# Routing in four groups and a slot table in DRAM: a graph layer with a mixture of experts on one Trainium2 core

## The chip, the core and the metric

The kernel runs on one core of a Trainium2 chip. A core has engines with an instruction queue each: TensorE (PE, whose weight loads the profile lists as PEld), VectorE (DVE), ScalarE (ACT), GpSimd (POOL) and SyncE (SP), and 16 DMA engines. The metric is the time of one execution on the device, in microseconds; of several executions the median is taken.

## What is computed

6250 nodes carry 256 features each. With `xn` the layer-normed input, the kernel adds three things to `x`:

```
x = x + gnn(xn, src, dst) + mix(xn)        # 206250 edges; mix: linear attention, 8 heads
x = x + ffn(layernorm(x))                  # mixture of 8 experts, capacity 977 each

# in ffn
logits = x @ gate_w + gate_b
idx    = argmax(softmax(logits));  prb = that probability
pos    = (cumsum(one_hot(idx), axis=0) * one_hot).sum(-1) - 1      # place within the expert
kept   = pos < C
buf[idx, pos] = x ;  y = relu(buf @ w1 + b1) @ w2 + b2
out    = y[idx, min(pos, C-1)] * (prb * kept)
```

Only the part that finds `idx`, `prb` and `pos` of each node, and the table from an expert's slots back to nodes, is what follows calls **routing**. `pos` is a running count over all nodes, so routing has an order.

## The kernel before, in words

Nodes lie in 49 blocks of 128; two blocks are a **pair** (`q`), 24 pairs and a last block of 106. The program has three stages: one with layer norm, keys and values and the degrees (to about 375 us), the **main stage** (about 378 to 1119 us), and the experts (from about 1140 us).

**Main stage.** For each destination block the neighbours' rows are summed by one-hot matrices. Each block takes 16 **slots**. In every slot PE builds four tiles (`build`, L1680, from marks that DVE wrote), ACT evacuates them (`tile_evac`, L1277), and PE sums the tiles of the block before with six or eight matmuls (`sum_up`, L1688). DVE writes the marks in four chunks per block (two instructions each at L1964), up to twelve slots before PE needs them; a ring holds them. In slot 2 of each block PE also transposes the next block's keys (`block_keys`, L1626), which makes these rows a clock of the stage: one per block.

Four blocks, those of the pairs 8 and 16 (`GATHERED`), are not summed by PE. GpSimd gathers their neighbours' rows by indirect DMA and lets the DMA add them up: per pair 56 rounds for two blocks, 112 DMAs, the first four without an addition (L974), the others with one (L976). All 224 stand back to back in GpSimd's queue. Four accumulators take turns, so that a gather waits only for the one four before it. DVE picks the sums up in `gathered` (L2251, L2255), in its fixed place. So 45 blocks remain on PE, at the positions 0 to 44, and DVE reaches pair 8's sums at position 18, pair 16's at position 32, each at slot 8 of the block.

Beside the blocks, each pair is **finished**: in slots 0 to 15 after its start (`first`) the mix matmuls (PE, L1554), scaling, bias and norm (DVE), in slots 16 to 31 (`second`) the second layer norm, its transposes (L1768) and the gate matmuls. `finish_starts` spaces the starts by 32 slots, but by 24 behind the gathered pairs, since two blocks less lie between them: pairs 8 to 12 and 16 to 20 come denser. This holds in the branch `sparse`, taken when no block has more than its share of edges; it is the one that runs here.

**Routing, per pair** (before):
- `choose` on DVE, seven instructions (L2393 to L2400): logits from the gate's PSUM, bias, maximum, difference, first best expert, one-hot.
- ACT's `exps` (L1357), with a load of its table.
- PE's `count` (L1786 to L1789): running counts by matmuls with a triangle of ones.
- `route` on DVE, sixteen instructions (L2415 to L2442): probability, position, slot number, and then one-hot rows of the slot's low and high part.
- PE's `place` (L1795): two matmuls spread node number and probability into a table `inv_ps` in PSUM.
- `add_slots` on DVE (L2409) adds this to `inv_acc`.

PE waits for `inv_added` before it writes keys to the PSUM bank that also holds `inv_ps` and `cum_ps`. All engines run in program order; a wait holds up what stands behind it.

**Tail.** Behind position 44, the last block and the last pair are routed together (three blocks wide, `last_route`). Then `inv_acc` gives the experts' lists of nodes.

## Time and profile before

| | us |
|---|---|
| median of 3 runs | 1460.66 |
| lowest, highest | 1456.71, 1464.74 |
| the profiled execution | 1463.94 |
| its span, first to last instruction | 1462.7 |
| PE, DVE, ACT, POOL busy | 1305.0, 1198.4, 934.8, 799.2 |
| granted TensorE clock, mean | 0.970 |

The busy share of an engine counts the modelled duration of each instruction. A matmul's includes its way through the array, and matmuls overlap, so that 98% busy does not mean full use. A stretch of the program is read better from the times between rows that come once per block. "Idle before <-" names what ended an engine's wait.

### The profile page before, as it was taken

How to read it: one execution, taken by the hardware profiler on the slowest of the kernel's cores; microseconds unless marked ns; L12 is line 12 of the kernel's file. 1: busy time of each engine (PE TensorE's matmuls, PEld its weight loads, DVE VectorE, ACT ScalarE, POOL GpSimd, SP SyncE). 2: the span in 40 equal slices, each digit the busy share in tenths (PEclk: the TensorE clock that was granted, in tenths of full speed). 3: DMA queues.
4: the chain of work that ended last, by engine and by line, in shares of the span. 5: the costliest groups of instructions: out<-in, count | busy, mean ns of one | idle time of the engine just before them, and what ended most of it. 6: DMA issues, size and time to landing. Idle time of an engine off the chain costs nothing. (4 is left out here: it accounts for less than half of the span.)

```text
span 1462.7 us, 38776 instructions
## 1 busy us (share of the span) xinstructions
PE 1305.0 (89%) x14051; PEld 1091.4 (75%) x14053; DVE 1198.4 (82%) x2455; ACT 934.8 (64%) x2122; POOL 799.2 (55%) x629
## 2 busy tenths in 40 slices
PE   4698888995879999998989998999999898989987
PEld 3355555562768888887878887888886687979986
DVE  7797888898869888998899888989984577767786
ACT  4486777776546676665756666657665556565754
POOL 5357445206238888888888884000000577676574
PEclk8799999997989999999999999999999999999999
DMA  9625431002826655666655664121114433343220
GB/s 301 209 57 118 93 77 37 29 23 93 255 64 114 120 99 99 99 99 131 107 105 122 108 101 75 38 73 38 38 38 138 126 118 122 95 136 116 74 79 25
DMA packets 96441, 145.71 MB, mean 100 GB/s; under 512 B 14249, under 2 KB 72262, under 8 KB 96123
## 3 DMA queue, kind: packets, MB, share of 16 engines
q0 software_dynamic: 46080, 69.85, 26.0%
q1 hardware_dynamic: 50186, 73.61, 15.1%
q8 instruction: 100, 1.64, 0.5%
q14 instruction: 75, 0.61, 0.2%
HBM read 105.08 MB, written 60.14 MB: 113 GB/s over the span
## 5 line engine op out<-in xcount | busy, mean ns | idle before, releaser
L1688 PE MATMUL bank<-reg_b,reg_a 128*128 128x256 f16 x4410 | 597.3, 275 | 8.5 <-ACT reg_a L1277 8.0
L1277 ACT ACTIVATE reg_a<-bank 128x392 f16<-128x392 f32 x720 | 343.0, 496 | 214.7 <-PE bank L1680 187.2
L1688 PEld LDWEIGHTS bank<-reg_b,reg_a 128*128 128x128 f16 x4410 | 396.8, 98 | 51.0 <-issue 10.2
L976 POOL DMA_INDIRECT reg_a<-h_rows,reg_d x216 | 395.1, 1829 | 66.2 <-issue 66.2
L1964 DVE TENSOR_TENSOR reg_c<-iota_v,reg_c 128x2048 f16<-128x2048 f16 (+1 forms) x282 | 368.2, 1321 | 45.3 <-ACT reg_c L1170 15.6
L1680 PE MATMUL bank<-reg_a,reg_c 128*128 128x98 f16 x2880 | 243.0, 209 | 16.1 <-ACT reg_a L1277 10.2
L1680 PEld LDWEIGHTS bank<-reg_a,reg_c 128*128 128x128 f16 x2880 | 200.4, 99 | 32.4 <-issue 17.4
L1964 DVE TENSOR_TENSOR reg_a<-iota_h,reg_c 128x1568 f16<-128x1568 f16 x180 | 174.3, 968 | 0.0
L990 POOL COPY take_idx<-inv_i 128x8 int32<-128x8 int32 (+1 forms) x8 | 1.7, 217 | 240.5 <-DVE inv_i L2515 240.5
L1920 PE MATMUL bank<-w_hi,hid_hi 128*128 128x256 f32 (+1 forms) x368 | 107.3, 292 | 12.1 <-DVE w_lo L2550 6.9
L1922 PE MATMUL bank<-w_hi,hid_lo 128*128 128x256 f32 (+1 forms) x368 | 104.6, 284 | 0.0
L1921 PE MATMUL bank<-w_lo,hid_hi 128*128 128x256 f32 (+1 forms) x368 | 104.5, 284 | 0.0
L1901 PE MATMUL bank<-xT_hi,w_hi 128*128 128x512 f32 (+2 forms) x240 | 85.5, 356 | 9.6 <-issue 5.5
L1035 POOL DMA_INDIRECT out<-reg_d,give_idx x60 | 71.7, 1195 | 40.8 <-issue 20.8
L1432 ACT ACTIVATE reg_d<-reg_d,slot_prb 128x256 f32<-128x256 f32 (+1 forms) x46 | 22.6, 506 | 103.2 <-DVE reg_d L2590 100.5
L2034 DVE TENSOR_REDUCE reg_e<-reg_e 128x16 f32<-128x1040 f32 x49 | 60.4, 1233 | 34.1 <-ACT reg_e L1148 32.2
L871 POOL DMA_INDIRECT reg_b<-in_dst,row_i x49 | 58.4, 1193 | 54.0 <-PE bank L1484 26.2
L995 POOL DMA_INDIRECT reg_b<-tok_rows,take_idx x64 | 75.6, 1182 | 17.7 <-issue 11.5
L1902 PE MATMUL bank<-xT_lo,w_hi 128*128 128x512 f32 (+2 forms) x240 | 81.1, 338 | 0.0
L1903 PE MATMUL bank<-xT_hi,w_lo 128*128 128x512 f32 (+2 forms) x240 | 81.0, 338 | 0.0
L1920 PEld LDWEIGHTS bank<-w_hi,hid_hi 128*128 128x128 f32 (+1 forms) x368 | 70.0, 190 | 14.6 <-issue 4.9
L1554 PE MATMUL bank<-reg_w,xnT_t 128*128 128x512 f16 x300 | 73.1, 393 | 4.1 <-issue 1.9
(370 smaller groups left out, 2520.6 us busy)
## 6 DMA issues: line engine op xcount, KB each, us to landing
reg_b<-in_L_ffn_w SPq DMA_DIRECT2D x16, 1024.0 KB
h_rows<-reg_b POOLq DMA_DIRECT2D x14, 896.0 KB, 9.8
tok_rows<-reg_e SPq DMA_DIRECT2D x24, 512.0 KB
x_bias<-in_x SPq DMA_DIRECT2D x1, 6250.0 KB
x_bias<-b_out_rows POOLq DMA_DIRECT2D x10, 625.0 KB
x_t<-x_bias SPq DMA_DIRECT2D x24, 256.0 KB
xnT_t<-xnT_rows SPq DMA_DIRECT2D x24, 256.0 KB
out<-reg_e SPq DMA_DIRECT2D x24, 256.0 KB
```

Source lines behind the costliest of these rows:

```text
L976: ins = g.indirect_dma_start(out=acc[i % 2][m][k], out_offset=None, in_=h_rows, in_offset=at, compute_op=ALU.add)
L995: nc.gpsimd.indirect_dma_start(out=gx[k][:, c, :], out_offset=None, in_=tok_rows[:, :], in_offset=bass.IndirectOffsetOnAxis(ap=take_idx[k] ...
L1277: return a.activation(AT[k].rearrange("p h (w t) -> p h w t", w=2)[:, :, :, s * GROUP:(s + 1) * GROUP], tile_ps[bk][:, 0:GROUP * 2 * NB].r ...
L1680: ins = t_.matmul(tile_ps[bk][:, i * 2 * NB:(i + 1) * 2 * NB], lo_ring[c][:, s % CG * GROUP + i, :], hi_ring[c][:, s % CG * GROUP + i, :], ...
L1688: ins = t_.matmul(agg_ps[k][:, 0:D], AT[k][:, h, :], h_all[:, half, h, :], start=(first and h + half == 0), stop=(last and h == NB - 1 and ...
L1901: t_.matmul(bank[f % 4][:, 0:w], w1_hi[:, c, fs], xT_hi[:, c, at], start=(c == 0), stop=False)
L1902: t_.matmul(bank[f % 4][:, 0:w], w1_hi[:, c, fs], xT_lo[:, c, at], start=False, stop=False)
L1903: ins = t_.matmul(bank[f % 4][:, 0:w], w1_lo[:, c, fs], xT_hi[:, c, at], start=False, stop=(c == DC - 1))
L1920: t_.matmul(y_ps, hid_hi[:, f, at], w2_hi[:, f, :], start=(f == 0), stop=False)
L1921: t_.matmul(y_ps, hid_hi[:, f, at], w2_lo[:, f, :], start=False, stop=False)
L1922: ins = t_.matmul(y_ps, hid_lo[:, f, at], w2_hi[:, f, :], start=False, stop=(f == FC - 1))
L1964: return v_.tensor_tensor(out.rearrange("p t (v u) -> p t v u", u=2), iota.rearrange("p (v u) -> p v u", u=2).unsqueeze(1).to_broadcast(sh ...
```

## The change

- `choose` is cut down per pair: DVE only multiplies the gate's PSUM out into a buffer `logits` for all blocks (`gate_out`).
- The rest runs in four groups: pairs 0 to 7, 8 to 15, 16 to 21, and 22 alone. `group_choose` and `group_route` on DVE are instructions up to 16 blocks wide; ACT has one `exps` per group, PE one chain of counting matmuls. The first three groups stand at positions 19, 33 and 43 (`group_pos`): choose at slot 0, ACT's exp at slot 6, count and route at slot 8.
- `place` and `add_slots` per pair are gone, with the one-hot rows for them. In their place DVE computes a row number, and GpSimd writes for each block 128 rows of two numbers (node and probability, 8 bytes) to a table `slot_rows` in DRAM by an indirect DMA (`scatter`, 46 in all).
- GpSimd's 16 scatters of the first group stand inside the gathers of pair 16, those of the second and third behind the gathers, the last two in the tail.
- The table in DRAM is zeroed early from `inv_acc`; SP loads it back (`slot_tab`) once all scatters have landed, and `add_slots` adds it to the last three blocks' `inv_ps` once.

```diff
-FIN_STEPS = ROUTE_STEPS + MIX_STEPS + 6
+FIN_STEPS = MIX_STEPS + 1
+GROUP_STEPS = 17
+ROUTES = ((0, 8), (8, 16), (16, 22), (22, 23))
...
+GATHER_FROM = 40
+GATHER_SLOTS = 2.3
+SCATTER_LATE = 32
...
+    slot_rows = dram("slot_rows", (NE * CROWS, 2))
...
+    GROUP_AT = GroupAt(0, 6, 8, 8)
+    group_pos = [-(-(starts[q1 - 1] + 2 * SLOTS) // SLOTS) for _, q1 in ROUTES[:-1]]
...
     # SyncE
+        sp.wait_ge(inv_added, 1)
+        sp.dma_start(slot_rows.rearrange("(p c) w -> p (c w)", p=P), inv_acc[:, :]).then_inc(xb_in, 16)
...
         load_b2(0, 0)
+        sp.wait_ge(placed, 16 * 2 * (NQ - 1))
+        sp.dma_start(slot_tab, slot_rows.rearrange("(p c) w -> p c w", p=P)).then_inc(w_in2, 16)
         finished(NQ)
...
     # GpSimd
+        def scatter(b):
+            g.indirect_dma_start(out=slot_rows, out_offset=bass.IndirectOffsetOnAxis(ap=slot_row[:, b:b + 1], axis=0),
+                                 in_=token[:, b, :], in_offset=None, bounds_check=NE * CROWS - 1, oob_is_err=False
+                                 ).then_inc(placed, 16)
+
+        def group(i):
+            pool.wait_ge(slot_hot, i + 1)
+            for b in range(2 * ROUTES[i][0], 2 * ROUTES[i][1]):
+                scatter(b)
...
                 for j in range(GROUNDS):
                     for m in range(2):
+                        at_slot = GATHER_FROM + GATHER_SLOTS * ((i * GROUNDS + j) * 2 + m)
+                        if (scattered < len(ROUTES) - 1 and group_pos[scattered] * SLOTS + SCATTER_LATE < at_slot
+                                and (group_pos[scattered] + 1) * SLOTS < starts[q]):
+                            group(scattered)
+                            scattered += 1
...
+            for i in range(scattered, len(ROUTES) - 1):
+                group(i)
...
     # ScalarE
-            if s == 15:
-                exps(q)
+                def fin(s):
+                    if s == GROUP_AT.exps and p in group_pos:
+                        group(group_pos.index(p))
...
     # TensorE
-            if s == 5 and not first_pair(q):
-                pe.wait_ge(key_out, min(q * 2 + 5, NB) if isinstance(q, int) else q * 2 + 5)
-                pe.wait_ge(inv_added, q)
-                count(q - 1)
...
+        def group(i, keys=None):
+            w = 2 * (ROUTES[i][1] - ROUTES[i][0])
+            pe.wait_ge(key_out, min(keys or 2 * ROUTES[i][1] + 3, NB))
+            pe.wait_ge(route_hot, i + 1)
+            t_.matmul(cum_ps[:, 0:w, :], utri16[:, :], g_hot[:, 0:w, :], start=True, stop=False)
+            for d in range(1, w):
+                t_.matmul(cum_ps[:, d:w, :], ones16[:, :], g_hot[:, 0:w - d, :], start=False, stop=False)
+            t_.matmul(cum_ps[:, 0:w, :], ones16[:, :], g_routed[:, 0:w, :], start=False, stop=True).then_inc(route_cum, 1)
...
         def tail():
-            for s in (5, 6):
-                first(NQ - 1, s)
+            first(NQ - 1, 6)
+            group(len(ROUTES) - 1)
...
     # VectorE
             if c == 3:
                 dve.wait_ge(fin_gate, q + 1)
-                choose(q, q)
+                v_.tensor_tensor(logits[:, ds(q * 2, 2), :], gate_ps, mix_bc[:, D:DG].unsqueeze(1).to_broadcast([P, 2, NE]),
+                                 ALU.mult).then_inc(gate_out, 1)
...
+            group_step(v_.scalar_tensor_tensor(low, low, float(NE * CT), high, ALU.mult, ALU.add))
+            group_step(v_.tensor_tensor(slot_row[:, b0:b1], low, drop, ALU.add))
+            dve.sem_inc(slot_hot, 1)
...
+        def add_slots():
+            dve.wait_ge(w_in2, 96)
+            dve.wait_ge(slot_used, 2)
+            halves_ = inv_acc[:, :].rearrange("p (w c) -> p w c", w=2)
+            v_.tensor_tensor(halves_, slot_tab.rearrange("p c w -> p w c"),
+                             inv_ps.rearrange("p (w c) -> p w c", w=2), ALU.add).then_inc(inv_added, 1)
```

**Where instructions move.** GpSimd, the gathers of the main stage, before (the first two rows are pair 8, the others pair 16):

```order
L974 DMA reg_a<-h_rows,reg_d 128x256 x4
L976 DMA reg_a<-h_rows,reg_d 128x256 x108
L974 DMA reg_a<-h_rows,reg_d 128x256 x4
L976 DMA reg_a<-h_rows,reg_d 128x256 x108
```

And in the changed kernel, the same place:

```order
L1016 DMA reg_a<-h_rows,reg_d 128x256 x4
L1018 DMA reg_a<-h_rows,reg_d 128x256 x108
L1016 DMA reg_a<-h_rows,reg_d 128x256 x4
L1018 DMA reg_a<-h_rows,reg_d 128x256 x13
L970 DMA slot_rows<-reg_c 8192x2 x16
L1018 DMA reg_a<-h_rows,reg_d 128x256 x95
L970 DMA slot_rows<-reg_c 8192x2 x28
```

Sixteen scatters have come between the 17th and the 18th gather of pair 16, and 28 stand behind the last one.

DVE, position 19 of the changed kernel (L2009 are the marks, L2280 scales a block's sum), the choosing half of the first group:

```order
L2280 SCALAR_TENSOR_TENSOR reg_e<-bank,rin,norm_bc 128x256
L2445 COPY reg_c<-routed 128x128
L2446 TENSOR_TENSOR reg_c<-reg_c,gate_b_bc 128x128
L2447 TENSOR_REDUCE reg_c<-reg_c 128x16
L2448 TENSOR_TENSOR reg_c<-reg_c 128x128
L2450 SCALAR_TENSOR_TENSOR reg_c<-reg_c,rev 128x128
L2451 TENSOR_REDUCE reg_c<-reg_c 128x16
L2452 TENSOR_TENSOR reg_c<-rev,reg_c 128x128
L2454 TENSOR_REDUCE reg_c<-reg_c 128x8
L2455 TENSOR_TENSOR routed<-routed,reg_c 128x8
L2009 TENSOR_TENSOR reg_c<-iota_v,reg_c 128x2048
```

These nine stand between two chunks of marks; the eleven of the routing half stand two chunks later, before the last layer norm steps of pair 8. Before, 16 instructions of `route` stood in front of the norm of every pair.

## Rows read from the trace of the kernel before

**Rows 1.** Windows: length, busy us (x instructions) of PE, PEld, DVE, ACT, POOL; PEclk, DMA, GB/s.
```profile
600.00:650.00 50.00, 49.20 (x610) 44.75 (x609) 44.34 (x105) 34.39 (x74) 42.99 (x24) 1.00 0.73 111
700.00:750.00 50.00, 45.68 (x535) 40.96 (x533) 45.18 (x107) 32.82 (x72) 42.39 (x26) 0.97 0.62 118
```
**Rows 2.** Who waited for whom, 500 to 1100 us: us in total, times, longest.
```profile
PE bank L1680 <- ACT reg_a L1277: 7.7, 4, 2.2
...
ACT reg_e L1345 <- DVE reg_e L2352: 7.4, 4, 2.1
```
**Rows 3.** Groups by line: busy us, mean ns of one | idle us before them.
```profile
L976 POOL DMA_INDIRECT reg_a<-h_rows,reg_d x216 | 395.1, 1829 | 66.2 <-issue 66.2
...
L1035 POOL DMA_INDIRECT out<-reg_d,give_idx x60 | 71.7, 1195 | 40.8 <-issue 20.8
```
**Rows 4.** Timeline of DVE: the pick-up of the gathered sums of pairs 8 and 16.
```profile
668.42 0.43 DVE L2251 TENSOR_TENSOR reg_a<-reg_a 128x256 f32<-128x256 f32 x1 [3.24 <-issue]
...
901.06 0.43 DVE L2251 TENSOR_TENSOR reg_a<-reg_a 128x256 f32<-128x256 f32 x1 [2.60 <-DMA reg_a<-h_rows,reg_d]
903.43 0.43 DVE L2251 TENSOR_TENSOR reg_a<-reg_a 128x256 f32<-128x256 f32 x1 [1.94 <-DMA reg_a<-h_rows,reg_d]
```
**Rows 5.** Timeline of POOL: a gather, two plain ones, and the last of all.
```profile
617.06 1.54 POOL L976 DMA_INDIRECT reg_a<-h_rows,reg_d  x1 [0.31 <-issue]
...
663.99 1.71 POOL L974 DMA_INDIRECT reg_a<-h_rows,reg_d  x1 [0.30 <-issue]
666.00 0.95 POOL L974 DMA_INDIRECT reg_a<-h_rows,reg_d  x1 [0.30 <-issue]
...
895.93 1.92 POOL L976 DMA_INDIRECT reg_a<-h_rows,reg_d  x1 [0.31 <-issue]
```
**Rows 6.** Timeline of DVE, 600 to 635 us: start, length, line, operation.
```profile
605.40 0.17 DVE L2393 TENSOR_TENSOR reg_e<-bank,mix_bc 128x16 f32<-128x16 f32 x1 [0.88 <-PE bank L1554]
...
606.78 1.22 DVE L1964 TENSOR_TENSOR reg_c<-iota_v,reg_c 128x2048 f16<-128x2048 f16 x1
...
615.25 0.17 DVE L2415 TENSOR_REDUCE reg_e<-reg_e 128x2 f32<-128x16 f32 x1
...
618.63 1.22 DVE L1964 TENSOR_TENSOR reg_c<-iota_v,reg_c 128x2048 f16<-128x2048 f16 x1
...
624.48 0.25 DVE L2409 TENSOR_TENSOR inv_acc<-inv_acc,bank 128x128 f32<-128x128 f32 x1
```
**Rows 7.** Timeline of PE, 600 to 642 us, with three key rows.
```profile
608.24 0.25 PE L1626 MATMUL bank<-ident,reg_c 128*64 128x64 f16 x4
...
615.50 1.47 PE L1554 MATMUL bank<-mix_hl,xnT_t 128*128 128x256 f16 x12
616.80 0.34 PE L1680 MATMUL bank<-reg_a,reg_c 128*128 128x98 f16 x4
...
621.20 0.61 PE L1795 MATMUL bank<-reg_w 128*128 128x128 f32 x4
621.65 0.34 PE L1680 MATMUL bank<-reg_a,reg_c 128*128 128x98 f16 x4
...
624.79 0.25 PE L1626 MATMUL bank<-ident,reg_c 128*64 128x64 f16 x4 [0.72 <-DVE inv_acc L2409]
...
639.65 0.25 PE L1626 MATMUL bank<-ident,reg_c 128*64 128x64 f16 x4
```
**Rows 8.** Timeline of PE: key rows (L1626) of the positions 20, 24, 34, 38.
```profile
692.98 0.32 PE L1626 MATMUL bank<-ident,reg_c 128*64 128x64 f16 x4
...
764.67 0.25 PE L1626 MATMUL bank<-ident,reg_c 128*64 128x64 f16 x4 [1.30 <-DVE inv_acc L2409]
...
927.77 0.25 PE L1626 MATMUL bank<-ident,reg_c 128*64 128x64 f16 x4
...
999.99 0.25 PE L1626 MATMUL bank<-ident,reg_c 128*64 128x64 f16 x4 [1.30 <-DVE inv_acc L2409]
```
**Rows 9.** Timeline of DVE in the tail: scaling of the last block.
```profile
1121.29 0.48 DVE L2235 SCALAR_TENSOR_TENSOR reg_a<-bank,rin,norm_bc 128x256 f32<-128x256 f32 x1 [0.37 <-DVE reg_a L2361]
```

More of the change, by code:

```diff
@@ L512, in build @@
     gs_of = [g_s if q in (0, NQ - 2, NQ - 1) or q % 2 == 0 else g_alt for q in range(NQ)]
-    Places = namedtuple("Places", "mix count route place add")
-    KEYS_AT = 2
-    PLACES = {2: Places(9, 9, 8, 14, 12), 14: Places(9, 9, 8, 16, 16), 10: Places(9, 11, 12, 18, 20),
-              6: Places(9, 9, 8, 14, 12)}
+    KEYS_AT, MIX_AT = 2, 9
+    GroupAt = namedtuple("GroupAt", "choose exps count route")
+    GROUP_AT = GroupAt(0, 6, 8, 8)
+    group_pos = [-(-(starts[q1 - 1] + 2 * SLOTS) // SLOTS) for _, q1 in ROUTES[:-1]]
+    gs_of = [g_s if q in (0, NQ - 2, NQ - 1) or q % 2 == 0 else g_alt for q in range(NQ)]
+    KEYS_AT, MIX_AT = 2, 9
+    GroupAt = namedtuple("GroupAt", "choose exps count route")
+    GROUP_AT = GroupAt(0, 6, 8, 8)
+    group_pos = [-(-(starts[q1 - 1] + 2 * SLOTS) // SLOTS) for _, q1 in ROUTES[:-1]]
     def places_of(q):
-        return PLACES[(KEYS_AT - starts[q]) % SLOTS]
+        return Places(9, 11, 12) if (KEYS_AT - starts[q]) % SLOTS == 10 else Places(9, 9, 8)
     def active(p, s):
@@ L525, in active, with main_phase @@
         return [(q, at - starts[q]) for q in range(NQ - 1) if 0 <= at - starts[q] < 2 * SLOTS]
-    def main_phase(eng, gnn, prepare, first, second, tail, sparse, ahead=None):
+    def main_phase(eng, gnn, prepare, first, second, tail, sparse, group, ahead=None):
         def blocks(with_rounds):
@@ L541, in pairs @@
             pair(0)
-            with eng.Fori(1, NQ - 2) as q:
-                pair(q)
+            for i, (q0, q1) in enumerate(ROUTES[:-1]):
+                with eng.Fori(max(q0, 1), q1) as q:
+                    pair(q)
+                group(i)
             pair(NQ - 2)
@@ L1754, in first @@
                 ins.then_inc(fin_mix, 1)
-            if s == 14 and not first_pair(q):
-                place(q - 1)
         def second(q, s):
             w, o = blocks_of(q), fin_of(q)
-            if s == -1:
-                pe.wait_ge(inv_added, q + 1)
             if s == 10:
@@ L1822, in tail @@
             busy(7)
-            pe.wait_ge(route_hot, NQ)
-            t_.matmul(total_ps, ones16[:, :], routed[:, :], start=True, stop=False)
-            for m in range(3):
-                t_.matmul(total_ps, ones16[:, :], last_route.hot[:, m, :], start=False, stop=(m == 2))
-            count(NQ - 1, 3, last_route)
+            last_count()
             busy(12)
-            pe.wait_ge(inv_added, NQ)
-            place(NQ - 1, 3, last_route)
+            last_place()
             busy(30)
@@ L2328, in first @@
                 biased(q, *(sums or ()))
-                if not sums:
-                    slots_of_last(q)
+                n[0] = 0
             if c == 3:
-                if not first_pair(q) and not fixed(q, NQ) and not sums:
-                    add_slots(q - 1)
                 if not fixed(q, NQ):
@@ L2411, in route, with each @@
-        def route(p, q, w=2, o=pair_route):
+            def each(part):
+                return part.unsqueeze(2).to_broadcast([P, w, NE])
+            dve.wait_ge(gate_out, ROUTES[i][1])
+            v_.tensor_copy(g_routed[:, 0:w, :], wide(routed[:, :]))
+            group_step(v_.tensor_tensor(log, log, wide(gate_b_bc[:, :]), ALU.add))
+            group_step(v_.tensor_reduce(out=top, in_=log, op=ALU.max, axis=AX.X))
+            v_.tensor_tensor(diff, log, each(top), ALU.subtract).then_inc(route_d, 1)
@@ L2446, in tail @@
             link(v_.tensor_scalar(node_1[:, NB - 1:NB], node_1[:, NB - 1:NB], valid[:, :], None, ALU.mult))
-            for c in (0, 1, 3):
+            for c in (0, 1):
                 first(NQ - 1, c)
+            group(len(ROUTES) - 1)
+            first(NQ - 1, 3)
             for c in (0, 1):
@@ L2458, in tail @@
             dve.wait_ge(fin_gate, NQ + 1)
-            choose(NQ - 1, NQ, 3, last_route)
-            route(NQ - 1, NQ, 3, last_route)
-            add_slots(NQ - 1)
+            last_choose()
+            last_slots()
+            add_slots()
         def sparse():
@@ L2496, in fin @@
                             second(q, at // CG - CHUNKS, True)
-                        if at == places_of(q).add and q:
-                            add_slots(q - 1)
                 gnn(b, p % 2, fin, False, DENSE[p + 2] if p + 2 < len(DENSE) else None)
-        main_phase(dve, gnn, prepare, first, second, tail, sparse)
-        dve.wait_ge(inv_added, NQ + 1)
-        n_inv = [0]
+        main_phase(dve, gnn, prepare, first, second, tail, sparse, group)
+        dve.wait_ge(inv_added, 2)
+        n_inv = [len(ROUTES) * GROUP_STEPS]
         def chain(ins):
             n_inv[0] += 1
-            ins.then_inc(inv_dve, 1)
-            dve.wait_ge(inv_dve, n_inv[0])
+            ins.then_inc(slot_dve, 1)
+            dve.wait_ge(slot_dve, n_inv[0])
         in_slot = inv_acc[:, 0:NE * CT]
```

233 lines of the change are left out of this document (136 added, 97 removed).

## The prediction

> **What bounds the kernel now.** I read the windows of the main stage first, then one pair on DVE and on PE, then what GpSimd delivers and who waits for it.
>
> In a regular stretch PE is busy 49.2 of 50 us, DVE 44.3 [rows 1]. In the dense stretch behind a gathered pair PE falls to 45.7 of 50 while DVE rises to 45.2, and the granted clock to 0.97 of 2.4 GHz [rows 1]. So PE sets the pace where pairs start 32 slots apart, and where they start 24 apart DVE's lateness gets through: ACT waits for DVE's variances (L1345, up to 2.1 us) and PE for ACT's tiles (L1680, up to 2.2 us) [rows 2].
>
> A third engine matters. GpSimd's 224 gathers run without a gap: each takes 1.83 us, with 0.31 us of issue ahead of it, 2.13 us in all [rows 3]. DVE waits for them at both places where it picks up sums: 3.2 us for pair 8, until 668.4, and for pair 16 from 898.5 to 903.4, 2.6 and 1.9 us in two waits [rows 4]. The last gather left GpSimd at 897.85 and landed 5.6 us later [rows 4, 5]. So both meetings are already late by a little: **whatever DVE and PE gain ahead of a meeting is lost there, and whatever is put into GpSimd's queue ahead of the last gather moves the second meeting.**
>
> **What goes.** On DVE `choose` takes 1.38 us (605.40 to 606.78, seven instructions, 0.20 each) and `route` 3.38 us (615.25 to 618.63) [rows 6]. One instruction of `choose` stays; with `add_slots` 1.2 + 3.4 + 0.2 = 4.8 us go per pair, some 105 us over 22 pairs. On a regular pair that is worth nothing by itself, since PE paces it. PE loses `count` (five narrow matmuls, an estimated 0.13 us), `place` (0.45 us, 621.20 to 621.65) and its wait for `inv_added` before the keys (0.72 us, at 624.79): 1.3 us per regular pair [rows 7]. ACT loses an Exp and its table load per pair, hidden.
>
> **What comes.** A group costs DVE 20 chained instructions. Small ones are 0.20 us; the wide ones 0.25 to 0.30 us, as for L2409's 128 columns (0.25) [rows 6]: some 2.4 us for choosing and 2.6 us for routing. PE gets 17 narrow matmuls, an estimated 0.5 us, ACT one table load there and back. For the third group DVE has lead enough, so only PE's 0.5 us count. The first and second stand at positions 19 and 33, right behind a meeting, when DVE has no lead: their 5 us use up the 4.8 us that pair 8 (or 16) no longer costs there. So I take the time from the meeting to the key row of position 20 (668.4 to 693.0) as it is, less 0.5 us, and likewise from the second meeting to position 34 (903.4 to 927.8) [rows 4, 8]. PE will wait at slot 8 of these positions for the first one-hots; the same wait was ACT's and PE's before.
>
> **The dense stretches, behind the groups.** Positions 20 to 24 take 71.7 us [rows 8]. A regular pair with its two positions takes 31.4 us (608.24 to 639.65), 30.1 without its 1.3 us [rows 7]. Four positions with two pairs would be 60.2 us; at 24 slots apart it is two thirds of a pair more, whose matmuls (mix 1.30 us [rows 7], gates and transposes an estimated 0.7) add 1.3: 61.5 us. DVE, with 4.8 us less per pair, needs about 0.84 us per slot against PE's 0.95, so PE paces; I leave 1.0 us for waits and take 62.5 us: 9.2 us gained. Positions 34 to 38 (72.2 us) gain the same.
>
> **The sum, against the profiled execution (1463.94 us).**
> 1. Up to 668.4 us: seven pairs gain 9.1 us, and all of it goes into a longer wait of DVE at the first meeting. 0.
> 2. Position 20 to 24: −9.2. Position 24 to 32: four pairs at 1.3, and 0.6 more where the wait was 1.30 (764.67): −5.8 [rows 8]. With item 1's 0 DVE is at the second meeting 15.0 us earlier, 883.5 instead of 898.5 us.
> 3. GpSimd: 16 scatters inside pair 16's gathers. **This price the trace does not show**; nearest is the indirect store of 128 rows in the expert stage, 1.20 + 0.30 = 1.50 us [rows 3]. Lower bound: a plain gather with DVE at rest, 0.95 + 0.30 = 1.25 us; upper bound: a gather with addition, 2.13 us [rows 3, 5]. At 1.50 they are 24.0 us, and the last gather would be issued at 921.9.
> 4. But DVE then stands still from 883.5. A gather that no marks disturb takes 1.54 us instead of the mean 1.83; a plain one took 1.71 us under marks and 0.95 in DVE's wait [rows 3, 5]. Spacing 1.84 instead of 2.13 is 0.136 less: 38.4 us shrink by 5.2, and the longer first wait gives 1.0. The second meeting comes 24.0 − 5.2 − 1.0 = 17.8 us later, at 921.
> 5. Behind it: −9.2 to position 38; to the end 3.5 pairs at 1.3 and a wait of 0.5: −5.0; the third group's matmuls +0.5.
> 6. Tail: PE waits about 2.7 us for the one-hots of pair 22 before it sums the last block, but DVE comes to scale that block about 2 us after PE is done, held by its own work [rows 9]: +0.3. The reload of the table (64 KB) hides behind the expert's weights: 0; if the last scatters landed late, the experts would start late by as much.
>
> 17.8 − 9.2 − 5.0 + 0.8 = **+4.4 us: 1468.3 for the profiled execution**, which stands 3.3 us above the median; for the median 1460.66 + 4.4 = **1465 us**. With s for a scatter's price the sum is 13.8 × s − 16.4: it turns at s = 1.19 us, gives +1 at 1.25, and is over +0.5% (7.3 us, what a measurement of this kernel can tell) from s = 1.71; at 2.13 it is +13.
>
> **A rule against the trace.** During `route` (615.25 to 618.63) GpSimd is not slowed: the gather that starts at 617.06 takes 1.54 us [rows 5, 6]. The Trainium skill (SBUF — State Buffer, the note on the "DVE blocks DMA" trap in "two separate sides") says that GpSimd cannot write descriptors while DVE holds the port pair they share, and gives about 0.62 us for such a DMA alone and 3.1 us beside a DVE copy. It agrees with item 4, and speaks against scatters amid marks: by its 3.1 us they would be 50 us, an estimate from that page; the trace's plain gather under marks lost 0.8 us against the one at rest, not 2.5 [rows 5].
>
> **Rivals.**
> - **A, slower: the scatters cost as the gathers with addition.** Sixteen at 1.71 to 2.13 us and more, because they fall at 696 to 730 us, where DVE writes marks densely, or because the small writes delay the landings of the gathers behind them. +7 to +13, 1468 to 1474. It decides from 1.71 us. For it: 1.71 us for a plain gather under marks [rows 5]. Against: the mean of 60 stores, 1.20 us. Chance 0.2.
> - **B, faster: the scatters cost GpSimd little**, since each moves 1 KB where a gather moves 128. At s = 0.3 to 0.7 the sum is −12 to −7, about 1451. For it: nothing moves twice through memory. Against: a plain gather at rest still takes 0.95 us, and no indirect DMA in the trace less [rows 5]. Chance 0.12.
> - **C, faster: the lighter DVE lets GpSimd gather faster throughout.** If routing held it up as marks do (15% of the time before 898, 0.29 of 1.83 us), 11 us would go: −7, about 1454. Against: the undisturbed gather during `route`. Chance 0.08.
> - **The change does not do what it says:** the three groups on DVE take as long as the 22 pairs. They cannot: some 15 against 105 us.
>
> **How the numbers follow.** My case has 0.6: 1461 to 1468 by the scatter's bounds up to 1.71, and ±4 us for the stretches that I estimated. Of it I count 0.13 as slower by over 0.5% and 0.01 as faster, the rest within. A adds 0.2 to slower, B and C 0.14 to faster and 0.06 within. Faster 0.15, within 0.5% 0.52, slower 0.33. The range takes in B's and A's middles: 1450 to 1476.
>
> **What would show it.** In the new profile: 16 scatters between 696 and about 720 us, their mean and gap; gathers ending near 916 instead of 898; DVE's wait at the first meeting about 12 us, at the second about 38, with PE idle some 30 us before 924; gathers at 1.54 us meanwhile; the key row of position 24 near 755, of 38 near 1008; regular pairs 1.3 us shorter, without L1626 waiting. I am wrong if DVE does not wait for GpSimd at position 32, or if the gathers end where they ended before.

## The result, and the profile after

The change takes **1477.49 us** (median, 1476.61 to 1478.74); the kernel before took 1461.97 us in the same measurement (1456.71 to 1464.74). The ratio is 1.011, 95% interval 1.008 to 1.014: slower by 15.5 us, where +4.4 was forecast, and just outside the range (1450 to 1476). The profiled execution spans 1475.4 us against 1462.7, its mean granted clock is 0.950 against 0.970.

The page of the change, busy time and the slices:

```profile
span 1475.4 us, 37910 instructions
PE 1311.6 (89%) x13895; PEld 1085.5 (74%) x13896; DVE 1122.9 (76%) x2007; ACT 886.7 (60%) x2065; POOL 851.4 (58%) x675
PE   5688999986899999988799996899988899989987
PEclk8799999996999999999799997899999999999999
```

A slice is 36.9 us. PE falls to 7 tenths, from 8 in the slice before, and the clock to 0.7, in the one that begins at 701 us; the 6 at 885 us holds the second meeting, and the 8 behind it (922 to 959 us) a second fall that no meeting explains. The windows of the main stage, as in [rows 1], and then the stretches around two places that the forecast did not have (length, busy us of PE, PEld, DVE, ACT, POOL; PEclk, DMA share, GB/s):

```profile
600.00:650.00 50.00, 50.00 (x615) 45.60 (x613) 38.36 (x69) 31.12 (x74) 42.46 (x25) 1.00 0.63 115
700.00:750.00 50.00, 38.74 (x405) 31.73 (x404) 32.05 (x59) 22.95 (x53) 42.08 (x27) 0.79 0.47 84
...
692.00:707.00 15.00, 7.11 (x42) 3.37 (x41) 5.62 (x12) 2.35 (x8) 11.65 (x12) 0.67 0.02 1
707.00:718.00 11.00, 4.48 (x22) 2.23 (x22) 1.58 (x2) 2.77 (x6) 9.17 (x7) 0.50 0.43 58
...
945.00:956.00 11.00, 6.77 (x44) 3.57 (x43) 3.37 (x4) 1.52 (x5) 7.74 (x7) 0.71 0.02 2
```

In a regular stretch all is as forecast: PE is full, DVE is down from 44.3 to 38.4 of 50 us. But from 692 to 718 us PE issues 64 matmuls in 26 us, where it has 211 in the 18 us that follow. DVE and ACT are mostly idle with it (7.2 and 5.1 us busy of the 26), and until 707 us the DMA engines too (0.02); only GpSimd works. PE's timeline there (start, length, line, operation, idle time before it and what ended it):

```profile
700.58 0.24 PE L1733 MATMUL bank<-reg_a,reg_c 128*128 128x98 f16 x1 [1.00 <-issue]
700.62 0.41 PE L1741 MATMUL bank<-reg_b,reg_a 128*128 128x256 f16 x1
702.00 1.01 PE L1741 MATMUL bank<-reg_b,reg_a 128*128 128x256 f16 x4 [0.96 <-issue]
703.47 0.37 PE L1741 MATMUL bank<-reg_b,reg_a 128*128 128x256 f16 x1 [0.46 <-issue]
704.18 0.24 PE L1733 MATMUL bank<-reg_a,reg_c 128*128 128x98 f16 x1 [0.34 <-issue]
705.59 0.24 PE L1733 MATMUL bank<-reg_a,reg_c 128*128 128x98 f16 x1 [1.17 <-issue]
707.01 0.24 PE L1733 MATMUL bank<-reg_a,reg_c 128*128 128x98 f16 x1 [1.17 <-issue]
```

Many matmuls come singly, 0.71 us or twice that apart, and for nearly all of the gaps the profile shows nothing that holds them: "issue", not a semaphore. I read this as a PE that gets its instructions late; that is an inference, which the instruction packets further down fit but do not settle. I call such a stretch a **spell**. The change has three (692 to 718, 946 to 956, 1097 to 1108 us), and each lies in or just behind one of the three bursts of scatters on GpSimd (686.2 to 707.1, 931.4 to 954.7, 1090.7 to 1106.9 us). The first outlasts its burst by 11 us. Two scatters of the first burst:

```profile
686.23 1.06 POOL L970 DMA_INDIRECT slot_rows<-reg_c  x1 [0.30 <-issue]
...
706.12 0.98 POOL L970 DMA_INDIRECT slot_rows<-reg_c  x1 [0.30 <-issue]
```

The key rows of positions 20, 21, 34, 35 and 38, which answer to [rows 8] (L1626 is L1679 now):

```profile
680.28 0.32 PE L1679 MATMUL bank<-ident,reg_c 128*64 128x64 f16 x4
718.99 0.32 PE L1679 MATMUL bank<-ident,reg_c 128*64 128x64 f16 x4
...
934.61 0.25 PE L1679 MATMUL bank<-ident,reg_c 128*64 128x64 f16 x4
959.83 0.26 PE L1679 MATMUL bank<-ident,reg_c 128*64 128x64 f16 x4
...
1005.58 0.25 PE L1679 MATMUL bank<-ident,reg_c 128*64 128x64 f16 x4
```

And the second meeting, DVE's pick-up of pair 16's sums ([rows 4]; there 898.5 to 903.4):

```profile
908.44 0.43 DVE L2296 TENSOR_TENSOR reg_a<-reg_a 128x256 f32<-128x256 f32 x1 [14.28 <-DMA reg_a<-h_rows,reg_d]
910.30 0.43 DVE L2296 TENSOR_TENSOR reg_a<-reg_a 128x256 f32<-128x256 f32 x1 [1.43 <-DMA reg_a<-h_rows,reg_d]
```

### The profile page after: what moved, and what is told of

Read it like the earlier page. It is cut to its first block and busy times, and to the rows that moved or that the text cites. A ratio compares the mean times of both kernels' runs of the same rounds, so it can differ in the third digit from the quotient of the medians.

```text
span 1475.4 us, 37910 instructions
## 1 busy us (share of the span) xinstructions
PE 1311.6 (89%) x13895; PEld 1085.5 (74%) x13896; DVE 1122.9 (76%) x2007; ACT 886.7 (60%) x2065; POOL 851.4 (58%) x675
## 5 line engine op out<-in xcount | busy, mean ns | idle before, releaser
L1741 PE MATMUL bank<-reg_b,reg_a 128*128 128x256 f16 x4410 | 604.8, 276 | 19.6 <-issue 13.5
L2009 DVE TENSOR_TENSOR reg_c<-iota_v,reg_c 128x2048 f16<-128x2048 f16 (+1 forms) x282 | 368.2, 1321 | 117.0 <-PE bank L1733 81.8
L1018 POOL DMA_INDIRECT reg_a<-h_rows,reg_d x216 | 390.6, 1808 | 67.7 <-issue 64.6
L1733 PE MATMUL bank<-reg_a,reg_c 128*128 128x98 f16 x2880 | 246.9, 210 | 20.3 <-issue 9.7
L2009 DVE TENSOR_TENSOR reg_a<-iota_h,reg_c 128x1568 f16<-128x1568 f16 x180 | 174.1, 967 | 0.0
L970 POOL DMA_INDIRECT slot_rows<-reg_c x46 | 49.9, 1085 | 191.2 <-DVEq L2476 178.1
L1485 ACT ACTIVATE reg_d<-reg_d,slot_prb 128x256 f32<-128x256 f32 (+1 forms) x46 | 22.7, 506 | 104.5 <-DVE reg_d L2682 102.2
L1607 PE MATMUL bank<-reg_w,xnT_t 128*128 128x512 f16 x300 | 76.8, 408 | 4.1 <-issue 2.1
```

What stands on the lines that cost most here:

```text
L1018: ins = g.indirect_dma_start(out=acc[i % 2][m][k], out_offset=None, in_=h_rows, in_offset=at, compute_op=ALU.add)
L1607: ins = t_.matmul(out_ps, left[:, lx, m, c * P:(c + 1) * P], right(lw, c), start=(n + c == 0), stop=(n == 2 and c == DC - 1))
L1733: ins = t_.matmul(tile_ps[bk][:, i * 2 * NB:(i + 1) * 2 * NB], lo_ring[c][:, s % CG * GROUP + i, :], hi_ring[c][:, s % CG * GROUP + i, :], ...
L1741: ins = t_.matmul(agg_ps[k][:, 0:D], AT[k][:, h, :], h_all[:, half, h, :], start=(first and h + half == 0), stop=(last and h == NB - 1 and ...
L2009: return v_.tensor_tensor(out.rearrange("p t (v u) -> p t v u", u=2), iota.rearrange("p (v u) -> p v u", u=2).unsqueeze(1).to_broadcast(sh ...
```

## The experiments

**Two theories.** S: while GpSimd issues scatters in a burst, PE gets its instructions late. G: the group's own work holds PE (the new wait for the gate product, L1607 behind DVE's L2420, 21.1 us in two waits; the group's matmuls; its DVE chain). The first four runs went to one chip, on which the kernel before took 1462.38 us, as in the measurement above; I call it the first chip and take both for the same kind. (Which chip the measurement ran on is not known.)

**Without the scatters of groups 0 to 2.** SP then waits for the last two scatters alone. This leaves the slot table empty but for the last pair, so the experts gather and scatter other rows.

```
         def group(i):
             pool.wait_ge(slot_hot, i + 1)
-            for b in range(2 * ROUTES[i][0], 2 * ROUTES[i][1]):
-                scatter(b)
+            if i == len(ROUTES) - 1:
+                for b in range(2 * ROUTES[i][0], 2 * ROUTES[i][1]):
+                    scatter(b)
```

> The changed kernel without the 44 scatters of the first three groups (the 2 of the last group stay), so the slot table holds only the last pair's entries; everything else on all engines is as in the change. Theory S (while a burst of scatters runs, PE gets its instructions one at a time, 0.7 or 1.4 us apart, and the three bursts at 686, 931 and 1091 us cost about 20, 7 and 7 us): the spells of PE 'issue' gaps at 692-717, 946-955 and 1097-1108 us vanish, position 20 takes about 19 us instead of 38.7, and the time comes to about 1440 to 1450 us. Rival G (the group's own work holds PE: its new wait for the gate product, the group's matmuls and its DVE chain): position 20 still takes over 30 us and the time stays over 1465 us.

Measured: 1439.29 us, 0.984 of before (0.980 to 0.987), 38 us below the change. No issue gap over 0.15 us is left on PE from 380 to 1190 us, and PE is full behind the first meeting (687 to 705 is position 20):

```profile
687.00:705.00 18.00, 18.00 (x210) 16.02 (x208) 13.46 (x25) 10.41 (x25) 15.26 (x10) 0.91 0.65 131
...
PE bank L1608 <- DVE reg_c L2421: 21.8, 2, 14.4
```

The wait that G blames (here L1608 <- L2421) is as long as in the change (21.8 us against 21.1), and costs nothing new: it is the wait for pair 16's sums seen from PE. G falls. Set side by side, in us from key row to key row (the last column is the change on another chip, below):

| | before | change | no scatters | change, chip without spells |
|---|---|---|---|---|
| start to the first key row | 381.5 | 374.8 | 380.4 | not compared |
| positions 20 to 24 | 71.7 | 85.5 | 62.9 | 62.5 |
| 24 to 32 | 125.1 | 119.2 | 119.2 | 119.2 |
| 32 to 33 (second meeting) | 20.0 | 31.6 | 31.9 | 57.8 |
| 34 to 38 | 72.2 | 71.0 | 62.5 | 63.3 |
| 38 to 43 | 77.1 | 74.2 | 74.2 | 74.2 |
| 43 to the end | 385.6 | 395.6 | 383.6 | 381.6 |

**The table shows something that the sizes of the spells hide.** The first one (21.7 us: position 20 takes 38.7 us against 17.0) is the longest and costs next to nothing. The 16 scatters push the gathers' end back by 22 us relative to the run without them: from the first gather (417.84 and 424.44 us) to the end of the last it is 489.5 us against 467.6. The last gather of the change, then of the run without scatters:

```profile
905.81 1.57 POOL L1018 DMA_INDIRECT reg_a<-h_rows,reg_d  x1 [0.30 <-issue]
```
```profile
890.46 1.54 POOL L1019 DMA_INDIRECT reg_a<-h_rows,reg_d  x1 [0.30 <-issue]
```

PE and DVE would have waited those 22 us at position 32 to 33. They lost them at position 20 instead, and DVE's wait at the meeting is 14.3 us with them and 14.5 without. From the key row of position 20 to that of 33 the change takes 22.4 us more than the run without scatters, which is the gathers' delay and no more. The second and third spell have nothing behind them that waits. The second costs 8.5 us. Behind the third the table shows 12.0 us: 10.4 of them are there at the next wait that both runs have (PE for the one-hots of the last routing, 42.0 us behind the key row of position 43 against 31.6), and 1.6 come later, in the tail and the experts, where the two runs do not do the same work.

**Each scatter waits for the landing of the one before.**

```
                 scatter(b)
+                pool.wait_ge(placed, 16 * (b + 1))
```

> The change, with each scatter waiting until the one before has landed. Theory S in the form that the rate of scatters matters (1.29 us apart now): with some 2.5 to 3 us between them the spells shrink or vanish, while group 0's burst on GpSimd grows from 21 to 40-48 us, so the gathers end some 20 us later and DVE waits at the second meeting: 1465 to 1485 us, but position 20 at 19 to 25 us. If any scatter in flight starves PE, whatever the rate, the spells grow with the burst: over 1490 us. Rival G: position 20 stays at 38.7 us.

Measured: 1499.75 us, 1.028 (1.023 to 1.033). Scatters come 3.4 us apart, and on the same chip there is no spell at all. PE through the whole first burst:

```profile
682.00:741.00 59.00, 59.00 (x730) 53.81 (x729) 48.97 (x88) 38.15 (x90) 23.94 (x18) 1.00 0.24 69
...
DVE reg_a L2297 <- DMA reg_a<-h_rows,reg_d: 75.6, 4, 64.4
```

Positions 34 to 38 take 63.3 us here, with group 1's scatters beside them, in place of the change's 71.0. So a scatter in flight is not enough to starve PE; it takes scatters that follow closely. Whether their rate counts or how many are in flight at once, this run cannot tell, since pacing changes both. The price is on GpSimd: the gathers end at 935.2, and DVE waits 64.4 us for them. A second price comes at the end: the last scatter leaves GpSimd at 1165.8 us, and PE waits 12.8 us for the experts' first rows (L1930 on `reg_b<-tok_rows,take_idx`), so that from the key row of position 43 to the end this run takes 397.8 us without any spell.

**A burst in the kernel before**, first 16 scatters of 8-byte rows to a spare table, then 16 gathers of 8-byte rows, after the 24th gather of pair 16 (in the change the scatters stand after the 17th).

```
+        def burst():
+            for b in range(16):
+                g.indirect_dma_start(out=spare_rows, out_offset=bass.IndirectOffsetOnAxis(ap=spare_at[:, b:b + 1], axis=0),
+                                     in_=spare_in[:, b, :], in_offset=None, bounds_check=P * 64 - 1, oob_is_err=False
+                                     ).then_inc(spare_done, 16)
...
+                        if (i, j, m) == (1, 12, 0):
+                            burst()
```

> The kernel before with nothing changed but a burst of 16 scatters of 8-byte rows (constants to a spare table in DRAM) put into pair 16's gathers at the same place, 24 gathers in. Theory S: PE shows a spell of issue gaps of 0.7 us and its multiples soon after the burst starts, and a position takes 30 to 39 us in place of 19; the gathers end 21 us later; 1475 to 1490 us. Rival G: no spell; only the gathers' delay of 21 us less some faster gathers shows at the second meeting: 1465 to 1480 us, with all dense positions up to 32 within 1 us of before.

> As the run with the burst in the kernel before, but 16 gathers of 8-byte rows from DRAM into SBUF in place of the 16 scatters. If it is the small writes to DRAM that hold up PE's instructions (theory S, form W): no spell. If any 16 indirect DMAs that follow on one another without a wait and carry little data do it (form R, GpSimd's descriptors at 1.3 us each): the same spell as with the scatters, a position of 30 to 39 us.

Measured: 1481.32 us, 1.013 (1.010 to 1.017), and 1477.94 us, 1.012 (1.009 to 1.016). With scatters one position takes 24.8 us in place of 17.5, with one gap of 3.1 us on PE; with small gathers position 21 takes 29.0 in place of 15.9. In the second, PE is not alone. Who waited, 704 to 734 us, where "remote" is a wait for which the trace has no releaser on this core:

```profile
ACT reg_a L1295 <- remote: 11.1, 4, 5.2
PEld bank L1706 <- issue: 9.9, 5, 8.5
PE bank L1706 <- ACT reg_a L1295: 8.4, 1, 8.4
DVE reg_e L2411 <- remote: 5.9, 1, 5.9
```

So no group is needed, and no write to DRAM: 16 small indirect DMAs in a row are enough for PE to lose time on this chip. The losses here are smaller than the change's first, and in the second most of it is one wait for ACT, which itself waits for something the trace does not name; I don't know why. The total is again the gathers' delay. With scatters positions 20 to 24 take 8.6 us more than before and the stretch from 32 to 33 takes 14.2 more, together 22.8, where the gathers take 23.3 us longer from the first to the last; with small gathers it is 12.1 and 9.1, together 21.2, and the gathers take 21.2 longer.

**Late and paced, two in flight, interleaved, and a burst of 16 rows.** These four went to another chip, on which before took 1425.23 us.

```
-SCATTER_LATE = 32
+SCATTER_LATE = 10000
...
             for b in range(2 * ROUTES[i][0], 2 * ROUTES[i][1]):
+                if i == 2 and b > 1:
+                    landed_but(b, 0)
                 scatter(b)
+                if i < 2:
+                    landed_but(b, 1)
```

(Even and odd scatters count on two semaphores, and SP waits for both; `landed_but` waits for the scatter two before, or for the one just issued.)

> The change with the scatters of groups 0 to 2 all behind GpSimd's gathers (after 892 us), those of groups 0 and 1 each waiting until the one before has landed (3.4 us apart), those of group 2 with at most two in flight. Theory S (spells come only with scatters that follow on one another at 1.3 us, and their other cost is that they push back the gathers): no spell on PE, gathers end near 892 us as without scatters, the pace of 3.4 us ends group 1 before group 2 is chosen at 1072 us: 1439 to 1447 us, against 1462 before and 1477 for the change. Rival T (the slot table on the last pair's path costs what the spells didn't): 1450 to 1460 us though no spell is left.

Measured: 1408.42 us, 0.987 (0.984 to 0.990). It beats both kernels.

```
+                if b > 1:
+                    landed_but(b, 0)
                 scatter(b)
```

> The change with at most two scatters in flight, where about 2.6 are now, so that they follow at some 1.7 to 2.0 us in place of 1.29. Theory S, form rate (the spell comes from the rate of the small DMAs; gathers at 1.83 us make none): the spells are gone or under 3 us of issue gaps, position 20 takes 18.5 to 21 us, group 0's burst 27 to 32 us, gathers end near 915 us: 1455 to 1465 us. Form flight (two in flight are already enough to starve PE): spells stay, position 20 over 30 us, 1475 to 1490 us.

Measured: 1438.66 us, 1.007 (1.005 to 1.009); burst 32.2 us, gathers' end 892.4, no spell.

```
+                        if pending:
+                            scatter(pending.pop(0))
                         k = j % GACC
```

> The change with group 0's scatters put singly after each of 16 gathers, rather than all 16 in a row; groups 1 and 2 stay bursts. Theory S, form rate: scatter and gather together take about 1.3 + 1.85 us, so small DMAs come at 1.6 us on average and only every second is small: the first spell vanishes or falls under 3 us of gaps, position 20 takes 18.5 to 21 us, the spells of groups 1 and 2 stay at 7 us each: 1458 to 1465 us. If the 16 scatters starve PE wherever they stand: a first spell of the same 14 us of gaps, spread over 30 to 40 us, and 1475 us or more.

Measured: 1432.09 us, 1.004 (1.002 to 1.005). Position 20 takes 17.6 us, but the spells of groups 1 and 2, whose bursts this kernel leaves alone, are missing too.

```
-                g.indirect_dma_start(out=spare_rows, out_offset=bass.IndirectOffsetOnAxis(ap=spare_at[:, b:b + 1], axis=0),
-                                     in_=spare_in[:, b, :], in_offset=None, bounds_check=P * 64 - 1, oob_is_err=False
+                g.indirect_dma_start(out=spare_rows, out_offset=bass.IndirectOffsetOnAxis(ap=spare_at[0:16, b:b + 1], axis=0),
+                                     in_=spare_in[0:16, b, :], in_offset=None, bounds_check=P * 64 - 1, oob_is_err=False
```

> The kernel before with the burst of 16 scatters again, but each of 16 rows (partitions 0 to 15) in place of 128. If what starves the engines is the number of single 8-byte transfers or descriptors (form D): no spell, only the GpSimd time of the burst, 1465 to 1475 us. If it is the number of indirect DMAs that GpSimd issues in a row (form I): the same or a longer spell than with 128 rows, since each takes GpSimd the same 1.3 us or less; 1478 us or more.

Measured: 1448.11 us, 1.014 (1.011 to 1.017), without a spell. A scatter of 16 rows takes GpSimd nearly as long as one of 128 (groups by line, this kernel and then the burst with 128 rows on the first chip):

```profile
L954 POOL DMA_INDIRECT spare_rows<-reg_c x16 | 17.2, 1078 | 4.9 <-issue 4.9
```
```profile
L954 POOL DMA_INDIRECT spare_rows<-reg_c x16 | 19.1, 1192 | 4.9 <-issue 4.9
```

It tells nothing of the spells, since on this chip the change's own bursts make none. What it does show: 22 us more in GpSimd's queue cost the kernel before 1.4% where there is no spell, about as much as with one on the first chip (1.3%). This agrees with the sums above: there too the spell was hidden in the gathers' delay.

**The change again, with three of the others beside it.** That two bursts made no spell called for the change itself on such a chip.

> The change itself, unaltered, beside the others on this chip. The last four runs were on a chip on which the kernel before took 1425 us in place of 1462, and there even the unaltered bursts of groups 1 and 2 (1.3 us apart) made no spell. Theory C (the spells need the bursts and a chip on which PE's instructions come late): where before takes about 1462 us, the spells are back at all three bursts and the ratio is 1.008 to 1.014; where it takes about 1425 us, no spell, position 20 under 21 us, the gathers' delay alone is left: ratio 0.995 to 1.005. Rival N (the change has spells on any chip, and groups 1 and 2 missed them by luck): position 20 takes over 30 us, ratio over 1.008 on either chip.

Measured, on a third chip (before 1426.94 us): 1432.51 us, **1.0035 (1.002 to 1.005)**, no spell. DVE's pick-up at the second meeting:

```profile
887.82 0.42 DVE L2296 TENSOR_TENSOR reg_a<-reg_a 128x256 f32<-128x256 f32 x1 [40.65 <-DMA reg_a<-h_rows,reg_d]
889.44 0.42 DVE L2296 TENSOR_TENSOR reg_a<-reg_a 128x256 f32<-128x256 f32 x1 [1.19 <-DMA reg_a<-h_rows,reg_d]
```

Here the gathers' delay stands at the meeting, unhidden: 40.65 us in place of 14.28. Beside DVE at work the 16 scatters of group 0 took longer (groups by line, 600 to 900 us):

```profile
L970 POOL DMA_INDIRECT slot_rows<-reg_c x16 | 21.4, 1337 | 4.9 <-issue 4.9
```

That is 1.34 + 0.30 us each, against 1.02 + 0.30 in the first burst on the first chip.

The third burst can be laid side by side, since GpSimd waits for DVE's row numbers before both. Its 12 scatters take GpSimd 16.2 us on the first chip (1090.7 to 1106.9), with a spell, and 16.2 us here (1062.1 to 1078.4), with none. The first, the second and the fifth of each, first chip first:

```profile
1090.69 1.40 POOL L970 DMA_INDIRECT slot_rows<-reg_c  x1 [136.01 <-DVEq L2476]
1092.40 0.98 POOL L970 DMA_INDIRECT slot_rows<-reg_c  x1 [0.30 <-issue]
...
1096.27 1.65 POOL L970 DMA_INDIRECT slot_rows<-reg_c  x1 [0.30 <-issue]
```
```profile
1062.14 1.40 POOL L970 DMA_INDIRECT slot_rows<-reg_c  x1 [127.18 <-DVEq L2476]
1063.84 0.98 POOL L970 DMA_INDIRECT slot_rows<-reg_c  x1 [0.30 <-issue]
...
1067.70 1.65 POOL L970 DMA_INDIRECT slot_rows<-reg_c  x1 [0.30 <-issue]
```

So the rate of the scatters is the same, and something else decides whether PE starves. I call it the chip, but the runs do not separate the chip from the time at which they ran: the two sets with 1462 us for the kernel before are also the two earliest, and the first chip was not measured again.

> At most two scatters in flight, as before. Theory S, form rate, on a chip with spells: their gaps under 3 us, position 20 at 18 to 21 us, and 10 to 25 us faster than the change; on a chip without: equal to the change or up to 8 us slower, since the burst takes GpSimd 32 us in place of 21. Form flight: spells stay on a chip that has them, and it is as slow as the change or slower.

> All scatters behind the gathers, paced. Theory: 0.985 to 0.990 of the kernel before on any chip, no spell, gathers not pushed back; on a chip with spells about 35 us faster than the change, on one without about 15 us. Rival T (what helped was the chip): 0.995 or more where before takes 1462 us.

> Group 0's scatters one after each gather, groups 1 and 2 as bursts. On a chip with spells: by form rate none at the first burst (position 20 at 18 to 21 us) but the two of groups 1 and 2 at about 7 us each; if every scatter starves PE, gaps of 10 us or more between 685 and 745 us. On a chip without spells: as the change within 4 us.

Measured: 1.006 (1.004 to 1.008), 0.987 (0.985 to 0.989) and 1.002 (1.001 to 1.003). Late and paced, DVE waits 18.2 us at the meeting, and the time is 1409.36: 23.2 us below the change on the same chip, which is what 16 scatters inside the gathers cost: they take 26.0 us of GpSimd's time, and from the first gather to the end of the last it is 493.4 us against 469.6.

**Was it there before?** On the first chip, yes. PE's waits from 120 to 200 us, where neither kernel has a scatter to the slot table: the kernel before there, then the kernel before with the 16-row burst on the second chip (L1484 is L1502 there).

```profile
PE bank L1484 <- issue: 6.1, 13, 0.5
...
L1484 PE MATMUL bank<-reg_c 128*64 128x98 f16 x384 | 13.8, 213 | 6.1 <-issue 6.1
```
```profile
PE bank L1597 <- DVE reg_e L2064: 1.5, 7, 0.2
...
L1502 PE MATMUL bank<-reg_c 128*64 128x98 f16 x480 | 13.2, 206 | 0.0
```

On the first chip PE lost 6.1 us of 80 there to "issue" and got through 384 of these matmuls; on the second it lost none and got through 480. The last of these matmuls starts at 323.4 us on the first chip and at 290.3 on the second: this first stage makes 33 of the some 37 us between 1462 and 1425.

The stretch is not free of small indirect DMAs. GpSimd issues 34 others there (the kernel before on the first chip):

```profile
L888 POOL DMA_INDIRECT reg_d<-src_pad,edge_i x18 | 20.3, 1125 | 8.5 <-issue 4.3 <-PE bank L1554 3.1 <-POOL edge_i L882 1.1
L871 POOL DMA_INDIRECT reg_b<-in_dst,row_i x16 | 17.1, 1072 | 10.0 <-PE bank L1554 5.7 <-issue 4.2
```

They come in runs of two to five, and each of PE's "issue" gaps in these 80 us ends inside such a run or within 0.8 us behind it: behind the runs that end at 165.6, 170.9, 177.0 and 183.6 us, for instance, gaps end at 165.0, 171.5, 177.7 and 184.3. On the second chip there are 38 of them and no gap. So the first stage fits the same account as the spells; no run took these DMAs away or spaced them.

**The instructions themselves.** The DMA view of 690 to 718 us counts instruction packets of 16 KB (queue 8). The change on the first chip, then the run without scatters there:

```profile
DMA packets 1140, 0.65 MB, mean 23 GB/s; under 512 B 519, under 2 KB 1140, under 8 KB 1140
q0 software_dynamic: 1140, 0.65, 18.1%
```
```profile
DMA packets 3309, 3.58 MB, mean 128 GB/s; under 512 B 316, under 2 KB 2866, under 8 KB 3304
q8 instruction: 3, 0.05, 0.7%
```

None in 28 us against three, and the kernel before has two in the same window. The Trainium skill (Runtime: NRT & Kernel Launch, "Instruction fetch mechanics") says that an engine's sequencer fetches blocks of 16 KiB, 256 instructions, over a DMA queue of its own while it works on the block before, and that this is mostly hidden. The packets have that size; whether the fetch stays hidden in the spells no run shows. Whether the missing block is the cause or the effect the views do not tell: a PE that works off its block slowly also asks for the next one late.

**Six more runs on three chips**, to settle whether an intermediate rate makes a spell on a chip that has them. All three were of the other kind (before 1425.6, 1429.2 and 1426.7 us). The kernels are those above, and one that puts group 0 singly after gathers, group 1 by landing and group 2 two in flight.

> At most two scatters in flight. If this call lands on a chip on which the kernel before takes about 1462 us (the kind with spells): form rate says issue gaps under 3 us, position 20 at 18 to 21 us and a ratio of 0.997 to 1.004; form flight says spells of the change's size or more and 1.011 or over. If before takes about 1426 us: 1.005 to 1.008, as in the two runs there.

> Group 0's scatters singly behind gathers, groups 1 and 2 as bursts. On the kind of chip with spells: form rate says no first spell, but those of groups 1 and 2, ratio 0.995 to 1.004; if each scatter starves PE, gaps of 10 us or more while group 0 is scattered, ratio 1.010 or over. On the other kind 1.001 to 1.005.

> All scatters behind the gathers and paced by their landing. 0.984 to 0.990 of the kernel before on either kind of chip, and no spell. If on the kind with spells PE is starved while these scatters run at 3.4 us apart: gaps between 900 and 1010 us and a ratio over 0.993.

> Group 0's scatters singly after 16 gathers of pair 16, group 1's each after the landing of the one before, group 2's with at most two in flight: three rates in one kernel. On a chip with spells (before about 1462 us): form rate says no spell at groups 0 and 1 and under 3 us of gaps at group 2, ratio 0.988 to 1.000; if each scatter starves PE, gaps of 10 us or more at group 0 and about 7 at group 2, ratio 1.006 or over. On a chip without: as the interleaved run, 1.000 to 1.005.

> All scatters behind the gathers, paced. On a chip with spells (before about 1462 us): 0.984 to 0.990 and no issue gaps while they run; if scatters 3.4 us apart starve PE there, over 0.993. On a chip without: 0.984 to 0.990 again.

> Three rates in one kernel (group 0 singly after gathers, group 1 by landing, group 2 two in flight). On a chip with spells: form rate says no spell at groups 0 and 1 and under 3 us of gaps at group 2, ratio 0.988 to 1.000; if each scatter starves PE, 1.006 or over. On a chip without: 1.000 to 1.005.

Measured, in this order: 1.009 (1.006 to 1.012), 1.004 (1.002 to 1.005), 0.988 (0.985 to 0.991), 1.003 (1.001 to 1.005), 0.987 (0.983 to 0.990), 1.005 (1.003 to 1.007). No spell in any of them. Late and paced is thus at 0.987 to 0.988 on four chips; on the first kind of chip it has not run. The trace of the paced run there speaks for it (no gap at 3.4 us apart), but group 2's two in flight remain untried there, and so does every mean spacing between 1.5 and 3.4 us.

## Why the prediction was wrong, by its own steps

- **What bounds the kernel: right.** PE paces regular pairs, GpSimd the two meetings, and what is put ahead of the last gather moves the second.
- **Item 1 (up to the first meeting, 0): off by 4 us.** In the run without scatters, whose main stage starts within 1.1 us of before's, the key row of position 20 is at 687.69 against 692.98: 4.2 us gained. The gathers run faster: from the first to the end of the last it is 467.6 us in place of 472.5. That is a part of rival C. DVE's wait at the first meeting, forecast at about 12 us, is 7.1 + 1.4 us in the change's trace on the first chip.
- **Item 2: right to 1 us.** Positions 20 to 24 −8.8 without scatters, −9.2 on the chip without spells and −10.0 with paced scatters (forecast −9.2), 24 to 32 −5.9 in every trace of the changed kernel (−5.8). The third group's and both early groups' DVE work cost nothing that can be seen, as said.
- **Items 3 and 4: right for chips without spells.** 16 scatters took 26.0 us there, 1.62 each (1.34 + 0.30), and 20.9 us in the change's trace on the first chip, 1.3 each, where DVE stood still for most of the spell (forecast 1.50, bounds 1.25 to 2.13). DVE's wait at the meeting: 40.65 us (forecast about 38). The formula 13.8 × s − 16.4 gives +6.0 at 1.62; the change measured +5.6 against before on that chip. Without any scatter ahead of the last gather it gives −16.4; late and paced measured −16.8 to −17.8 on four chips. Part of this agreement is luck: the 4 us that item 1 missed are made up by a larger delay at the meeting. From the key row of position 20 to that of 33 the change takes 239.5 us on the chip without spells, 22.6 more than the trace of before on the first chip, where items 2 to 4 sum to +17.8.
- **Item 5: the step that failed.** "Behind it: −9.2 to position 38; to the end −5.0; third group +0.5" let the 28 scatters of groups 1 and 2 run on an idle GpSimd at no cost, because nobody waits for them. Without scatters positions 34 to 38 gain 9.7 and 38 to 43 gain 2.9, as forecast; with them, in the trace of the measurement, the two spells cost 8.5 and 10.4 us. From the first key row to the end the change's trace is 19.3 us longer than before's: 4.4 as forecast, −4.2 for item 1 and 18.9 for the two spells make 19.1. (It began its main stage 6.6 us earlier. That is not the change's doing: on the first chip the traces of either kernel begin it at 374.5 to 375.6 us or at 380.4 to 383.1.) That the bursts of groups 1 and 2 make the two spells is shown by taking them away and by pacing them, on one chip; why a burst starves PE, and why only there, stays open.
- **The forecast's own signs did not find the fault.** DVE does wait for GpSimd at position 32 (14.3 us, forecast about 38) and the gathers end later; what was missing is a sign for time that PE loses with no wait behind it.
- **Rival A had the sign and not the mechanism.** Scatters at 1.71 us or more would have made it slower; they were cheapest where the change was slowest.
- **The rule on the shared port.** By the 3.1 us beside a DVE copy that the Trainium skill gives (SBUF — State Buffer, "two separate sides") 16 scatters would be 50 us, an estimate. On the chip without spells, with DVE busy 22.7 of 27 us, they took 0.98 to 2.00 us each, and the mean is a third above the shortest. That the excess is DVE's doing is not shown; a factor of five is not there. The skill's figure is for a copy, and most of DVE's work here is `TENSOR_TENSOR`.
- **What I could have read.** The forecast took the change's time to be a matter of three queues. The trace of before had PE losing 6.1 us of 80 to "issue" in the first stage, which no wait explains, always in or just behind a run of small indirect DMAs. The forecast rests on no window ahead of 375 us.

## What to carry to other kernels

When gaps of the engine that sets the pace are put down to "issue", no wait explains them; look at what the other engines do at those moments. Here small indirect DMAs of an idle GpSimd, for which nobody waited, cost 19 us. Space such DMAs when nobody needs them soon, and check the last of them: paced to the end, they held the experts up by 12.8 us. In a queue that a meeting waits for, move everything that can be later behind it: with pacing, that turned +0.4% into −1.3% where there was no spell. And a long stall in front of a wait is not a loss by its length; subtract what the wait would have taken anyway.

## What the runs showed that was not expected

- The same kernel took 1462 us on the first chip and 1425 to 1429 us on five others, with no lower mean clock (0.965 to 0.972 against 0.964 to 0.974), and the change is worth 1.011 in the one place and 1.0035 in the other. Whether it is the chip or the time of the runs is not shown.
- On the first chip PE lost time beside 12 to 16 indirect DMAs of 8-byte rows in a row, 1.3 to 1.5 us apart on average, reads as well as writes; 3.4 us apart it lost none. On the other chips it lost none at 1.3 to 1.6 us.
- An indirect DMA of 8-byte rows costs GpSimd 1.19 us + 0.30 with 128 rows and 1.08 + 0.30 with 16.
- In a spell PE's clock falls to 1.2 GHz (0.50 in the window from 707 to 718 us), so the first matmuls after it run at half speed, 1.46 us for six sums where they take 0.82:

```profile
719.24 1.46 PE L1741 MATMUL bank<-reg_b,reg_a 128*128 128x256 f16 x6
```
